# Moved query products in a delta-rule stage and a reordered start of a cross-attention stage

## The reference

```python
q = silu(x @ Wq.T); k = silu(x @ Wk.T); v = x @ Wv.T      # reshaped to (b, n, 16, 32)
beta = 2.0 * sigmoid(x @ Wbeta.T)
k = k * rsqrt(sum(k * k, -1) + EPS)
# for each token: pred = k S; S = S + k (beta * (v - pred)); o = q S
og = o * sigmoid(x @ Wg1.T @ Wg2.T)
og = og * rsqrt(mean(og * og, -1) + EPS) * g_norm
x = layernorm(x + og @ Wo.T)
```

```python
q = (x @ Wq).reshape(b, n, 32, 16)
k, v = split(ctx @ Wkv, 2)                                # each (b, 512, 32, 16)
q, k = apply_axial_rope(q, pos), apply_axial_rope(k, pos)
attn = softmax(q k^T / sqrt(16)) @ v
x = layernorm(x + attn @ Wout + bout)
```

## Time and profile before

| what | value |
| --- | --- |
| median of 3 runs | 3118.55 us (3118.23 to 3125.44) |
| time of the profiled execution | 3114.41 us |
| its span on the core | 3112.6 us |
| mean granted TensorE clock in it | 0.914 of full |
| PE busy | 2642.7 us (85%) |
| DVE busy | 1901.2 us (61%) |
| ACT busy | 1464.0 us (47%) |
| POOL busy | 1155.0 us (37%) |
| Delta: first chain step of round 0 to that of round 7 | 112.2 to 665.1 us |
| Cross: its first matmul, its first row maximum, its first exponential | 2274.62, 2317.84 and 2345.96 us |

### The profile page before, as it was taken

How to read it: one execution, slowest core, us unless ns; L and a number is a source line. 1 busy time by engine, 2 the same in 40 slices (tenths; PEclk the granted TensorE clock), 3 DMA queues, 4 the chain that set the end, 5 groups by cost and what they waited for, 6 DMA issues and landing times.

```text
span 3112.6 us, 50558 instructions
## 1 busy us (share of the span) xinstructions
PE 2642.7 (85%) x20154; PEld 1433.2 (46%) x20154; DVE 1901.2 (61%) x2978; ACT 1464.0 (47%) x2608; POOL 1155.0 (37%) x1072
## 2 busy tenths in 40 slices
PE   5898989886878776699989888988779999999788
PEld 3665656552323322488745444444433333333244
DVE  4233333334899999657436665666646666667377
ACT  3343424324566565343345362625415666666355
POOL 0444444432778776300052516143232232331000
PEclk8898989887989987899999989899878999999889
DMA  3222222223033140322252334243155544442301
GB/s 96 72 63 78 71 74 64 69 55 143 21 109 101 49 171 14 138 94 83 96 151 85 93 105 126 96 130 138 42 119 119 102 118 110 105 101 63 124 28 41
DMA packets 196766, 284.50 MB, mean 91 GB/s; under 512 B 84388, under 2 KB 86468, under 8 KB 195636
## 3 DMA queue, kind: packets, MB, share of 16 engines
q1 hardware_dynamic: 196532, 281.27, 30.7%
HBM read 192.08 MB, written 63.31 MB: 82 GB/s over the span
## 4 chain that ended last, share of the span: by engine, by line
PE 40%; DVE 10%; issue 4%; ACT 4%; POOL 2%; DMA 2%; SPq 1%; DVEq 0%; ACTq 0%; POOLq 0%
PE ps L236 8%; PE ps L3560 4%; PE ps L2018 4%; PE ps L3573 4%; PE ps L2029 4%; PE ps L3492 3%; PE ps L3509 2%; PE ps L3543 2%; PE ps L2684 1%; DVE arena L2947 1%; DVE arena L2945 1%; PE ps L1670 1%; PE ps L3497 1%; DMA d_parts<-cross 1%; PE ps L2692 1%
## 5 line engine op out<-in xcount | busy, mean ns | idle before, releaser
L236 PE MATMUL ps<-arena 128*128 128x512 f32 (+3 forms) x1296 | 482.9, 526 | 27.6 <-ACT arena L972 14.3
L3745 DVE TENSOR_REDUCE cross<-ps 128x1 f32<-128x512 f32 x512 | 327.5, 684 | 174.7 <-PE ps L3543 174.7
L1654 POOL TENSOR_TENSOR arena<-arena 128x1024 f32<-128x1024 f32 x128 | 305.8, 2392 | 119.6 <-DVE arena L1646 119.4
L3653 ACT ACTIVATE cross<-ps 128x512 f32<-128x512 f32 x512 | 276.7, 592 | 151.3 <-PE ps L3560 150.9
L236 PEld LDWEIGHTS ps<-arena 128*128 128x128 f32 (+2 forms) x1296 | 195.7, 156 | 266.1 <-issue 179.2
L1670 PE MATMUL ps<-arena 128*128 128x512 f32 x512 | 268.5, 666 | 38.4 <-POOL arena L1654 38.4
L1646 DVE TENSOR_TENSOR_SCAN arena<-ps,arena 128x1024 f32<-128x1024 f32 x128 | 291.4, 2277 | 9.1 <-ACT ps L1637 9.0
L1637 ACT ACTIVATE ps<-arena 128x511 f32<-128x511 f32 x256 | 165.0, 679 | 157.3 <-DVE arena L1646 157.0
L600 POOL TENSOR_TENSOR arena<-arena 128x31 f32<-128x31 f32 (+15 forms) x217 | 135.5, 625 | 262.2 <-DMA arena<-d_a 245.7
L1670 PEld LDWEIGHTS ps<-arena 128*128 128x128 f32 x512 | 105.6, 215 | 192.1 <-issue 124.9
L3560 PE MATMUL ps<-cross,cross 50*128 50x512 f32 x512 | 155.8, 506 | 26.3 <-ACT cross L3653 20.9
(11 more groups left out here) (359 smaller groups left out, 5153.2 us busy)
## 6 DMA issues: line engine op xcount, KB each, us to landing
arena<-d_bc SPq DMA_DIRECT2D x32, 1024.0 KB, 5.4
cross<-d_parts SPq DMA_DIRECT2D x192, 128.0 KB, 4.3
arena<-d_x SPq DMA_DIRECT2D x16, 1024.0 KB, 5.3
d_parts<-cross SPq DMA_DIRECT2D x32, 512.0 KB, 3.9
d_x<-arena SPq DMA_DIRECT2D x48, 256.0 KB, 2.6
arena<-in_D_wlm SPq DMA_DIRECT2D x12, 1024.0 KB, 6.4
d_signs<-arena SPq DMA_DIRECT2D x32, 256.0 KB
arena<-arena SPq DMA_DIRECT2D x64, 128.0 KB, 2.1
```

The lines of the kernel that those rows point to most:

```text
L236: ins = pe.e.matmul(ps[:m, :n], lhsT(k), rhs(k), start=(k == 0), stop=(k == chunks - 1))
L1654: pool.e.tensor_tensor(h, h, s.bc[turn % s.SLOTS][:, 1], ALU.mult).then_inc(*pool.up("scan_hC"))
L3653: act.e.activation(s.E[:, k % 2, j], s.rexp.bank((u, i)), ACT.Exp).then_inc(*s.rexp.empty(act, (u, i)))
L3745: dve.e.tensor_reduce(s.mx[:, u % 2, t, h:h + 1], s.rmax.bank((u, m)), AX.X, ALU.max, negate=True).then_inc(*s.rmax.empty(dve, (u, m)))
```

## The change

In `Delta`, for rounds with p even, the query products of pair n move out of the fill: `pe_queries` runs ahead of `pe_og` and `pe_keys`, and `act_queries` stands ahead of both square roots on ACT. `pe_og` moves ahead of `pe_keys`, and `act_og` ahead of `act_split_k`. The fill of such a round becomes V, G (now four pieces instead of two), PT, tokens, K, beta (now four pieces), a pause, g1. DVE takes the values and the causal masks at earlier steps. The rounds with p odd keep their order.

In `Cross`, the keys' projection of unit 0 comes first, then the tokens, then the angles (before: angles, tokens, queries, keys). SP swaps the keys of unit 0 first, then the queries, stores both parts of unit 0 one after the other, swaps q and k of unit 1, and only then reloads both; the load of `wo` and of the bias row moves behind that, ahead of the rest. POOL turns the keys of unit 0 and DVE the queries. From unit 1 on the order is unchanged.

```diff
@@ Delta.pe_all
-                s.pe_beta(pe, 0)
+                for _ in s.pe_beta(pe, 0):
+                    pass
             if back and p % 2:
                 s.pe_triangles(pe, p)
+            if front and p % 2 == 0:
+                for _ in s.pe_queries(pe, n):
+                    pass
+            if p >= 1 and p % 2 == 0:
+                s.pe_og(pe, p - 1)
             if front:
                 s.pe_keys(pe, n)
-            if p >= 1:
+            if p >= 1 and p % 2 == 0:
+                s.pe_out(pe, p // 2 - 1)
+            if p >= 1 and p % 2:
                 s.pe_og(pe, p - 1)
-                if p % 2 == 0:
-                    s.pe_out(pe, p // 2 - 1)
@@ Delta.pe_fill
-        for c in range(s.E):
...
-        if tokens:
-            yield from s.pe_tokens(pe, (n + 1) // 2)
+        if n % 2 == 0:
+            yield from s.pe_queries(pe, n)
         pe.e.wait_ge(*R.at_emptied(pe, ("g1", n // 2)))
...
                 ins = e.matmul(ps[:, t], s.g1[:s.HD, (2 * h + t) * P:(2 * h + t + 1) * P], s.wg2[:s.HD, cols], start=True, stop=True)
+                if n % 2 and t == 0:
+                    yield
...
+        if tokens:
+            yield from s.pe_tokens(pe, (n + 1) // 2)
         if n + 1 < s.PAIRS:
             yield from s.pe_k(pe, n + 1)
         if tokens:
-            s.pe_beta(pe, (n + 1) // 2)
+            yield from s.pe_beta(pe, (n + 1) // 2)
+            yield
             s.pe_g1(pe, (n + 1) // 2)
@@ Delta.act_all
+            if front and p % 2 == 0:
+                s.act_queries(act, n)
             if p >= 1:
                 act.e.wait_ge(*act.on("delta_og_squares", p - 1))
...
+            if p >= 1 and p % 2 == 0:
+                s.act_og(act, p - 1)
             if front:
                 s.act_split_k(act, n)
-            if p >= 1:
+            if p >= 1 and p % 2:
                 s.act_og(act, p - 1)
@@ Delta.act_queries (new; its lines come from act_fill)
+    def act_queries(self, act, n):
+        s, e, R = self, act.e, self.ring
+        if n >= 2:
+            act.e.wait_ge(*R.at_filled(act, ("o", n - 2, 1)))
+        for c in range(s.E):
+            act.e.wait_ge(*R.at_filled(act, ("Q", n, c)))
+            e.activation(s.QT[:, n % 2, c, :], R.bank(("Q", n, c)), ACT.Silu).then_inc(*R.empty(act, ("Q", n, c)))
@@ Cross.small
-        if s.unit(f) is not None and i != -1:
+        if f > 0 and s.unit(f) is not None and i != -1:
             items.append((("Rk", f), [7, 7]))
...
-        if starts:
+        if starts and nb:
             items += [(("ang", nb), [11])] + [(("xT", nb, t), [12 + t]) for t in range(T)]
+        elif starts:
+            items += [(("Rk", 0), [10, 10])] + [(("xT", 0, t), [11 + t]) for t in range(T)] + [(("ang", 0), [15])]
@@ Cross.sp_all (sp_keep and sp_unfold are the two halves of sp_stack)
         s.sp_one_rows(sp)
+        s.sp_swap(sp, 0, 0)
+        s.sp_keep(sp, 0, 1)
+        s.sp_keep(sp, 0, 0)
         for w in range(2):
-            s.sp_swap(sp, 0, w)
-        for f in range(s.AHEAD):
+            s.sp_swap(sp, 1, w)
+        for w in (1, 0):
+            s.sp_unfold(sp, 0, w)
+        s.sp_late(sp)
+        for f in range(1, s.AHEAD):
             for w in range(2):
                 if f + 1 < s.AHEAD:
                     s.sp_swap(sp, f + 1, w)
```

94 lines of the change are left out of this document (58 added, 36 removed).

## The result

The changed kernel takes 3093.42 us (median of 4 runs, 3089.97 to 3097.37) beside 3119.16 us for the kernel before in the same runs; the medians lie 25.7 us apart. The ratio is 0.9925, 95% interval 0.9901 to 0.9949, that is 23 us less (16 to 31). The profiled execution took 3089.97 us (span 3088.2, mean granted clock 0.922 where it was 0.914).

A forecast was written before the change was run, and what follows sets the result against it. PE, holding 40% of the span, was taken to lose time in waits, and SP's stores and reloads to set Cross's main-loop start. Delta 10 plus Cross 3 made 13 us: 3118.55 to 3105.5 us, range 3098 to 3116.

The forecast's parts named there:

- (1): Delta, ahead of chains 2, 4, 6: query product of 6.9 us fills PE's idle, root 4.8 later, Wo 0.9 earlier.
- (2): Delta's even chains: the chain gets only 1.4 us shorter, the tail behind it loses 4.6 us.
- (3): Delta: PE waits 1.7 us for ACT's query split in round 2, up to twice that in round 4.
- case C: Rival: idle only moves, doubled stalls bring half-clock steps; Delta gives 3, Cross 1, time 3114.5 us; chance 0.30.
- (4): Delta, behind rounds 2 and 4: inverse and DVE's unit keys limit the gain; round 2 gives 4.5 us, round 4 3.5.
- (5): Delta, round 0: root, keys and chain start 5.6 us later; chain and tail give back, 1 us net.
- (6): Cross start: keys first and both parts stored before reloads bring the first maximum 8 us earlier, within 2.
- (7): Cross start: late weights and bias delay the store of unit 1's queries by 6.3 us, leaving 3 us gain.
- Rival B: Late weights in Cross cost nothing: Cross gives 9.5 us, time 3099 us; chance 0.15.
- the conditions under which I said I would be wrong: Cross's first matmul to first exponential below 64 us, query product over 9, or Delta ending less than 5 sooner.

The follow-up runs named there:

- e15: Changed kernel with beta behind the chain again in rounds 0, 2, 4, its chain places filled with unread 256-column matmuls; ratio to the kernel before 0.9972.
- e5: Changed kernel, but in rounds with queries in front ACT splits both query tiles before it takes any sign; ratio to the kernel before 0.9945.
- e7: Changed kernel, but Cross loads wo and its bias row in the second iteration of the main loop; ratio to the kernel before 0.9933.
- e10: Changed kernel, but Cross stores and reloads the keys of unit 0 before it stores the queries' parts; 3082.49 us, one run.
- e11: e7 with the rows of the first maxima written behind the reload of unit 1's keys; ratio to the kernel before 0.9905.
- e12: Changed kernel with the changes of e6, e7 and e11 together; ratio to the kernel before 0.9824, 3061.49 us.
- e6: Changed kernel, but on ACT both square roots stand ahead of the queries' activations; ratio to the kernel before 0.9875, 3076.05 us.
- e13: Changed kernel with beta behind the chain again in rounds 0, 2, 4, its chain places filled with unread 16-column matmuls; ratio to the kernel before 0.9969.
- e9: Kernel before, nothing moved, with an unread product of the queries' size ahead of the unit keys in even rounds; ratio to the kernel before 0.9975.

## Why the prediction was right in its direction and wrong in its size

**Queries in front (1).** The idle ahead of chain 2 was forecast as 4 us in one piece, and is 5.22. The product takes 7.03 us (6.9 forecast), the root follows the second activation and a table load of 1.28, and the two pauses have become one. So the mechanism was right. But the sum booked only a Wo product that starts 0.9 us sooner in each round, and left Wo at its old length; full clock for it stood in a bound. The runs show the reverse: counted from the chain before it, Wo starts 0.3 us sooner in three rounds together, takes 5.6 us less (13.90 and 14.58 us in rounds 2 and 4 of the first profile instead of 16.17 and 16.78), and 1.4 us more come behind it. That is 7.4 us where 2.8 were forecast. **This is the first mis-sized term, 4.6 us.** My own rows showed two pauses, each followed by slow steps, and the change removed the one in front of Wo.

**The chain and the tail (2).** Right: 4.6 us a round were booked for the tail, 13.8 in three rounds, and e15 gives 12.2.

**The stall (3).** Right in place and kind: 2.13 and 0.57 us in round 2 where I had 1.7 in all, 2.09 and 0.90 in round 4. Slow steps follow it, which I had only in case C. Round 2 gave 1.3 us and not 3.6, and the slow end of the chain goes with that: the four changed profiles that have it in round 2 take 64.8 to 66.0 us from chain 2 to 3, the three without it 62.2 to 63.8. e5 shows that ACT's signs are owed somewhere: removing the stall there moves it to the tokens.

**What is late next (4).** Right for round 3: the inverse was in time (PE's L723 begins at 326.43 with no wait), and the chain's first copy follows the unit keys and the mask at once, at 335.44. Chain 7, behind round 6, still waits for the inverse:

```profile
646.18 3.64 PE L723 MATMUL ps<-arena 128*32 128x128 f32 x64 [9.92 <-DMA arena<-d_t]
```

**Round 0 (5).** Chain 0 was to start 5.5 us later and starts 1.5 later. The keys' transposes do come late, 96.39 instead of 93.83, but in six of the seven changed profiles the product ahead of them starts 2 us earlier, and in three of these it also takes 7.2 us instead of 8.2. In e7, where neither holds, the transposes come at 99.01, 5.2 us late as forecast, and still the chain starts at 115.5, only 3.1 late. **This is the second mis-sized term, 4.0 us.** Why round 0's products start up to 2 us sooner, and how much of the rest is the clock, is open.

**Cross (6), (7).** The first maximum was forecast 8 us earlier and came 8.5; the way to the exponential was to fall from 71.3 to 68 and fell to 66.8. Against the means of three (72.6 and 67.0) it is 5.7 us. The closeness of the first number is luck, for its reasons were wrong. Storing both parts first saves nothing (e10). Of the 8.5 us, 4.6 lie between the first matmul and the first raw queries, and some 2.5 of these are the clock (from the start of the queries' projection to its copy it takes 6.29 us before and 3.74 after). The other 3.9 lie between the raw queries and the first maximum (29.1 and 25.2 us). Keys first is the likely reason, but no run has it alone.

On the way to the exponential SP reaches the store of unit 1's queries 10.0 us sooner (8.1 forecast; 29.2 us behind the first matmul instead of 39.2), and the store lands 4.8 us later after its issue (5.3 forecast: 6.3 less 1 for idle engines). **This cost is put down to the wrong thing, and is the third mis-sized term:** of the 4.8 us only 2.0 are the weights, as e7 shows, and 2.8 the twelve reloads ahead of the store, which the sum had at nothing. The weights' own price was 6.3 in my sum and is 3.6. The rule of the Trainium skill (DMA: Bandwidth & Descriptors, Queues, rings and completion order), consumed in ring order on each engine, fits the runs. From the end of SP's twelve reload issues to the landing, after needs 12.8 us and e7 9.8 (12.6 to 15.1 in the nine profiles with the late load, 9.6 to 10.4 in e7, e11 and e12); the 3.0 between the two are near the 3.3 that I estimate for the load's bytes at 399 GB/s. My 6.3 was too high, not the rule.

**The rest.** The first two errors make 8.6 us. Against them stand the 2.3 that round 2's interval fell short and small differences elsewhere, so Delta gave 15.0 for 10. Delta's 15 and Cross's 5.7 make 20.7 us, where the runs give 23 to 26 with an interval of 16 to 31. What remains, 3 to 5 us, is within it; the first pair of profiles shows 4 of them in Ternary, by chance. Of the conditions under which I said I would be wrong none came true in the first trace: the distance is 66.8, the product 7.03, Delta 10 us sooner. They didn't test the sum. Rival B is not what happened either: the late weights have a price, and the gain beyond my sum is mostly Delta's. (B's 9.5 us for Cross should be 9.1 by its own terms, 8.1 and about 1; nothing hangs on it.) Most steps held in place and kind, and the total didn't, since I had taken the clock at zero gain and the late load at its full landing time.

The other page that I weighed, the Trainium skill's ScalarE: Activation LUTs (What ACT_TABLE_LOAD costs), with 2.66 us a switch, is not borne out as a whole: the load takes 1.28 us in after and in e6, and the next activation follows at once, so no drain shows.

## What to carry to other kernels

Count the pauses of TensorE and what runs behind each: here a pause was paid twice, once as idle time and once in slow steps. When two are joined to one, let the short work stand behind it. When work is moved into a gap, keep what the other engine does for it behind what others wait for: here two activations ahead of two roots cost more than the move of the queries gained. Price a load by its bytes and the rate of the engines, and not by its time to landing. And take several profiles of the same code before a difference of 10 us is divided among causes.

## What was not expected of the hardware

- The clock fell while PE was busy. In e13 PE has no gap from 324 to 331 us, and the granted clock is 1.00 until 328, 0.74 until 331 and 0.50, the lower level of 1.2 GHz, behind it; from 335 to 340, with PE busy 5.00 of 5.00 us with beta's 16-column products, it is still 0.50. In e15, where products of 256 columns stood in the chain ahead, the chain's end ran at full clock, and in round 2 the clock fell only behind 326 us, while PE did beta.
- Work that nobody needs can make a kernel faster: e9, 0.9975.
- The same Delta code starts chain 7 anywhere from 646.2 to 655.1 us.
- DVE and POOL hold each other up. The scaling of the outputs (1024 elements a lane) takes 2.57 us in after, where it begins 0.40 us behind a POOL operation of the same size and ends 1.1 us behind it; in the kernel before it takes 1.22. There it is POOL that pays: its step of 60 elements begins 0.18 us behind the scaling and takes 1.28 us instead of 0.38. In both cases the operation that began first keeps its time, and the other ends later. DVE and POOL after, then DVE and POOL before:

```profile
239.43 2.57 DVE L1243 TENSOR_TENSOR arena<-arena 128x1024 f32<-128x1024 f32 x1
```

```profile
239.03 1.89 POOL L601 TENSOR_TENSOR arena<-arena 128x1024 f32<-128x1024 f32 x1 [2.75 <-DMA d_t<-arena]
```

```profile
237.97 1.22 DVE L1206 TENSOR_TENSOR arena<-arena 128x1024 f32<-128x1024 f32 x1
```

```profile
238.15 1.28 POOL L600 TENSOR_TENSOR arena<-arena 128x60 f32<-128x60 f32 x1
```

- In the long runs of 32x32 products ahead of each chain PE stands still for up to 3.5 us with nothing in the profile that it waits for (2.96 us ahead of 269.20 in after, 3.51 in e6, 2.69 in the kernel before). It is there in both kernels and was not tried.
